# A graph network's fourth edge pass: one engine change per round, ten rounds per group, twelve buffers of gathered rows

## The reference, cut to what matters

```
proj_feat = (in_feat @ W_proj).reshape(n_nodes, n_head, d_out)
src_score = jnp.sum(proj_feat * a_src, axis=-1)
tgt_score = jnp.sum(proj_feat * a_tgt, axis=-1)
edge_score = leaky_relu(src_score[src_ind] + tgt_score[tgt_ind], negative_slope=0.2)
edge_score = jnp.exp(edge_score - jnp.max(edge_score))
neigh_sums = segment_sum(edge_score, tgt_ind)
att_per_edge = edge_score / (neigh_sums[tgt_ind] + 1e-16)
out_feat = segment_sum(proj_feat[src_ind] * att_per_edge[..., None], tgt_ind)
```

## Time and profile before

| what | value |
|---|---|
| median of 3 runs | 7075.83 us (7072.01 to 7086.69) |
| profiled execution | 7071.4 us, span 7069.7 us |
| busy in the span | TensorE 5276.6 us (75%), VectorE 4158.6 us (59%), GpSimd 4214.4 us (60%), ScalarE 2748.0 us (39%) |
| granted TensorE clock, mean | 0.883 |
| the pass `edges_3` | about 5848 to 6626 us of the span |

### The profile page before, as it was taken

The page is one execution under the profiler, slowest core; times in us unless marked ns, Lnnn a source line. Parts: engine busy times, 40 slices in busy tenths (PEclk is TensorE's granted clock), DMA queues, the critical chain, the costliest instruction groups (busy, mean ns, idle before and its releaser), DMA issues. The chain is left out here.

```text
span 7069.7 us, 108538 instructions
## 1 busy us (share of the span) xinstructions
PE 5276.6 (75%) x29030; PEld 3736.3 (53%) x29030; DVE 4158.6 (59%) x14866; ACT 2748.0 (39%) x6645; POOL 4214.4 (60%) x3907
## 2 busy tenths in 40 slices
PE   4776889788866665787699996766666675776788
PEld 3655677545455554333488874333333344555566
DVE  4454777523345555777488884544445454655698
ACT  0000555411111212666355554555555462222354
POOL 4664466666668886777644442455555445554598
PEclk9898999988888887999799998888888887888899
DMA  4554666444456666999545552333333332333466
GB/s 128 174 173 150 178 179 177 136 124 135 131 117 107 106 108 128 317 301 303 176 141 147 152 148 74 90 86 88 86 89 90 84 87 60 74 72 72 121 185 175
DMA packets 1163875, 966.37 MB, mean 137 GB/s; under 512 B 161046, under 2 KB 975586, under 8 KB 1163268
## 3 DMA queue, kind: packets, MB, share of 16 engines
q1 hardware_dynamic: 977956, 684.36, 32.2%
q0 software_dynamic: 163072, 210.16, 15.4%
q10 hardware_dynamic: 22240, 64.90, 2.5%
HBM read 485.30 MB, written 496.79 MB: 139 GB/s over the span
## 5 line engine op out<-in xcount | busy, mean ns | idle before, releaser
L2337 PE MATMUL l_nodes_f<-l_nodes_h_t_s,w_f 128*128 128x512 f32 x784 | 435.7, 684 | 433.4 <-ACT l_nodes_act_t L2289 422.9
L526 POOL DMA_INDIRECT tgt_tab<-l_nodes_ext,rank_at x392 | 389.9, 995 | 580.9 <-ACT l_nodes_ext L2312 474.0
L1556 POOL DMA_INDIRECT agg<-l_edges_b_rows,l_edges_b_at x392 | 608.5, 1552 | 133.9 <-issue 79.4
L1844 POOL DMA_INDIRECT l_edges_kv<-kv_tab,src_i x392 | 397.7, 1015 | 400.6 <-DVE l_edges_v_e L1865 291.2
L526 POOL DMA_INDIRECT to_col<-l_nodes_col_s,rank_row x392 | 415.4, 1060 | 326.6 <-ACT l_nodes_col_s L1250 232.3
L2510 POOL DMA_INDIRECT l_edges_proj<-proj_tab,src_i x392 | 382.3, 975 | 376.8 <-DVE l_edges_msg L2483 247.7
L435 POOL DMA_INDIRECT l_nodes_ag<-agg,sum_at x392 | 380.0, 969 | 241.4 <-issue 119.5
L961 POOL DMA_INDIRECT l_edges_fetched<-in_x,src_i x392 | 381.5, 973 | 218.8 <-DMA dst_i<-in_dst 111.0
L1314 POOL DMA_INDIRECT l_edges_a_at_row<-to_row,src_i x392 | 378.2, 965 | 219.0 <-issue 111.6
L526 POOL DMA_INDIRECT q_tab<-l_nodes_qkvs,rank_at x392 | 403.0, 1028 | 149.5 <-issue 105.9
L891 ACT COPY l_edges_rows<-l_edges_sums 128x264 f32<-128x264 f32 (+1 forms) x294 | 122.1, 450 | 947.9 <-DMA dst_i<-in_dst 463.7
(11 more groups left out here) (359 smaller groups left out, 14716.8 us busy)
## 6 DMA issues: line engine op xcount, KB each, us to landing
agg<-zeros ACTq DMA_DIRECT2D x98, 516.0 KB
l_nodes_xg<-x SPq DMA_DIRECT2D x196, 256.0 KB
kv_tab<-l_nodes_qkvs SPq DMA_DIRECT2D x98, 512.0 KB
agg<-l_edges_rows SPq DMA_DIRECT2D x98, 266.0 KB
l_nodes_ag<-agg SPq DMA_DIRECT2D x98, 266.0 KB
proj_tab<-l_nodes_ext SPq DMA_DIRECT2D x98, 264.0 KB
l_nodes_ag<-agg SPq DMA_DIRECT2D x98, 258.0 KB
l_nodes_ag_odd<-agg SPq DMA_DIRECT2D x98, 258.0 KB
```

What stands on the lines that cost most here:

```text
L526: pool.indirect_dma_start(table, bass.IndirectOffsetOnAxis(ranks[:, n * G + j:n * G + j + 1].bitcast(U32), 0), rows[:, j, :], None, bounds ...
L1556: pool.indirect_dma_start(agg1[j // 2], bass.IndirectOffsetOnAxis(at[k][:, j:j + 1].bitcast(U32), 0), rows[k][:, j, :], None, compute_op=A ...
L1844: pool.indirect_dma_start(kv[k][:, j, :], None, kv_tab, bass.IndirectOffsetOnAxis(src_i[:, n * G + j:n * G + j + 1].bitcast(U32), 0),).the ...
L2337: pe.matmul(f[m % 2][:], w_f1[:, m * P:(m + 1) * P], h_t_s[k][:], start=True, stop=True).then_inc(f_done, 1)
```

## The change

`edges_3` is rewritten with other lags and more buffers. No instruction that computes is added or removed; VectorE's, TensorE's, ScalarE's and GpSimd's counts for the pass stay the same.

- New lags: VectorE score 4, raise_top 5, lower 6, rest 1, one-hots 2, tail 2, marks, weigh and carry 7; TensorE total 8 (now first in its round), line 0, turn_top 4, spread_tgt 3, spread_top 5; ScalarE empty 9 (now first), line 1, middle 2, head 0, exponentials 6; SyncE's store 10.
- `proj` has twelve buffers (`DEEP`), and the gathers of group n wait for `weighed` of group n-12. `parts`, `lifted` and `msg` have four buffers, `both` one.
- VectorE's `weigh` loses its wait for `summed`; `spread_tgt` waits for `joined` of the group just before it rather than of the second before; the window's load waits for `rested` rather than `tgt_spread`.

```diff
-                proj = [sb(f"proj{k}", [P, G, D + H3]) for k in range(RING)]
-                parts = [sb(f"parts{k}", [P, G, 3, H3], BF16) for k in range(2)]
+                DEEP = 3 * RING
+                proj = [sb(f"proj{k}", [P, G, D + H3]) for k in range(DEEP)]
+                parts = [sb(f"parts{k}", [P, G, 3, H3], BF16) for k in range(RING)]
...
-                msg = [sb(f"msg{k}", [P, G, D + H3]) for k in range(2)]
+                msg = [sb(f"msg{k}", [P, G, D + H3]) for k in range(RING)]
...
                             dve.wait_ge(risen, n + 1)
-                            if follows(i, k, 2):
-                                dve.wait_ge(summed, n - 1)
-                            dve.tensor_tensor(msg[k % 2][:, :, 0:D].rearrange("p j (h c) -> p j h c", c=C3),
-                                              proj[k][:, :, 0:D].rearrange("p j (h c) -> p j h c", c=C3),
+                            dve.tensor_tensor(msg[k][:, :, 0:D].rearrange("p j (h c) -> p j h c", c=C3),
+                                              proj[n % DEEP][:, :, 0:D].rearrange("p j (h c) -> p j h c", c=C3),
...
-                        rotation(dve, groups, (1, take_rest), (2, score), (1, lambda i, k: mark_line(dve, i, k, tgt_spread)),
-                                 (1, take_tail), (2, raise_top),
-                                 (2, lambda i, k: mark(dve, i, k, (3, 2))), (2, lower), (2, lambda i, k: mark(dve, i, k, (1, 0))),
-                                 (2, weigh), (2, carry), loop=False)
+                        rotation(dve, groups, (4, score), (5, raise_top), (6, lower), (1, take_rest),
+                                 (2, lambda i, k: mark_line(dve, i, k, tgt_spread)), (2, take_tail), (7, lambda i, k: mark(dve, i, k)),
+                                 (7, weigh), (7, carry), loop=False)
...
-                            if reuses(i):
-
-                                pool.wait_ge(weighed, n - RING + 1)
+                            if n >= DEEP:
+
+                                pool.wait_ge(weighed, n - DEEP + 1)
                                 pool.sem_inc(pool_turn, 1)
...
-                            if follows(i, k, 2):
-
-                                pe.wait_ge(joined, n - 1)
+                            if follows(i, k, 1):
+
+                                pe.wait_ge(joined, n)
...
-                            if follows(i, k, 2):
-
-                                act.wait_ge(summed, n - 1)
+                            if n >= RING:
+
+                                act.wait_ge(summed, n - RING + 1)
...
-                        rotation(pe, groups, (2, turn_top), (0, lambda i, k: spread_line(pe, i, k)), (1, spread_tgt), (2, spread_top),
-                                 (3, total_messages), loop=False)
+                        rotation(pe, groups, (8, total_messages), (0, lambda i, k: spread_line(pe, i, k)), (4, turn_top),
+                                 (3, spread_tgt), (5, spread_top), loop=False)
...
-                        rotation(act, groups, (1, take_middle), (0, lambda i, k: copy_line(act, i, k)), (0, take_head), (2, rise), (2, ease_carry),
-                                 (3, lambda i, k: empty(act, i, k, low)), loop=False)
+                        rotation(act, groups, (9, lambda i, k: empty(act, i, k, low)), (1, lambda i, k: copy_line(act, i, k)), (2, take_middle),
+                                 (0, take_head), (6, rise), (6, ease_carry), loop=False)
...
-                        rotation(sp, groups, (0, lambda i, k: load_window(sp, i, k, tgt_spread)), (5, lambda i, k: store(sp, i, k)), loop=False)
+                        rotation(sp, groups, (0, lambda i, k: load_window(sp, i, k, rested)), (10, lambda i, k: store(sp, i, k)), loop=False)
```

More of the change, by code:

```diff
@@ L2413, in edges_3 @@
                 headed, rested, middled, tailed, joined = (sem(n) for n in ("headed", "rested", "middled", "tailed", "joined"))
-                proj_in = [[sem(f"proj_in{k}{j}") for j in range(G)] for k in range(RING)]
+                proj_in = [[sem(f"proj_in{k}{j}") for j in range(G)] for k in range(DEEP)]
                 with nc.Block() as block:
@@ L2448, in take_rest @@
                                 dve.wait_ge(tailed, n - 1)
-                            dve.tensor_tensor(rest[k % 2][:], tgt[k][:], parts[k % 2][:, :, 0, :], ALU.subtract).then_inc(rested, 1)
+                            dve.tensor_tensor(rest[k % 2][:], tgt[k][:], parts[k][:, :, 0, :], ALU.subtract).then_inc(rested, 1)
                         def take_tail(i, k):
@@ L2453, in take_tail @@
                             dve.wait_ge(middled, n + 1)
-                            dve.tensor_tensor(parts[k % 2][:, :, 2, :], rest[k % 2][:], parts[k % 2][:, :, 1, :],
+                            dve.tensor_tensor(parts[k][:, :, 2, :], rest[k % 2][:], parts[k][:, :, 1, :],
                                               ALU.subtract).then_inc(tailed, 1)
@@ L2521, in spread_tgt @@
                             pe.wait_ge(hot_made, n + 1)
-                            if follows(i, k, 2):
-                                pe.wait_ge(joined, n - 1)
+                            if follows(i, k, 1):
+                                pe.wait_ge(joined, n)
                             spread_rows(pe, lambda j: tgt_p[:, k % 2, j].rearrange("p s h -> p (s h)"), at_rank[k % 2],
-                                        parts[k % 2][:].rearrange("p t s h -> p t (s h)"), 3 * H3).then_inc(tgt_spread, 1)
+                                        parts[k][:].rearrange("p t s h -> p t (s h)"), 3 * H3).then_inc(tgt_spread, 1)
                         def turn_top(i, k):
@@ L2543, in total_messages @@
                             pe.wait_ge(weighed, place(i, k) + 1)
-                            total(pe, i, k, msg[k % 2])
-                        rotation(pe, groups, (2, turn_top), (0, lambda i, k: spread_line(pe, i, k)), (1, spread_tgt), (2, spread_top),
-                                 (3, total_messages), loop=False)
+                            total(pe, i, k, msg[k])
+                        rotation(pe, groups, (8, total_messages), (0, lambda i, k: spread_line(pe, i, k)), (4, turn_top),
+                                 (3, spread_tgt), (5, spread_top), loop=False)
                     @block.scalar
@@ L2553, in take_head @@
                             act.wait_ge(window_in[k], i * 16 + 16)
-                            if follows(i, k, 2):
-                                act.wait_ge(tgt_spread, n - 1)
-                            act.copy(parts[k % 2][:, :, 0, :], tgt[k][:]).then_inc(headed, 1)
+                            if n >= RING:
+                                act.wait_ge(tgt_spread, n - RING + 1)
+                            act.copy(parts[k][:, :, 0, :], tgt[k][:]).then_inc(headed, 1)
                         def take_middle(i, k):
@@ L2560, in take_middle @@
                             act.wait_ge(rested, n + 1)
-                            act.copy(parts[k % 2][:, :, 1, :], rest[k % 2][:]).then_inc(middled, 1)
+                            act.copy(parts[k][:, :, 1, :], rest[k % 2][:]).then_inc(middled, 1)
                         def rise(i, k):
@@ L2566, in rise @@
                             act.wait_ge(scored, n + 1)
-                            if follows(i, k, 2):
-                                act.wait_ge(summed, n - 1)
-                            act.activation(msg[k % 2][:, :, D:D + H3], lifted[k % 2][:], ACT.Exp, bias=low[k][:]).then_inc(risen, 1)
+                            if n >= RING:
+                                act.wait_ge(summed, n - RING + 1)
+                            act.activation(msg[k][:, :, D:D + H3], lifted[k][:], ACT.Exp, bias=low[k][:]).then_inc(risen, 1)
                         def ease_carry(i, k):
```

21 lines of the change are left out of this document (11 added, 10 removed).

## The result

The changed kernel takes 7126.22 us (median of 4 runs, 7119.97 to 7131.42) against 7073.92 us: 1.0072 of the kernel before, 95% interval 1.006 to 1.0085. It is slower, by 52 us; the forecast was 7034 us with a range from 6880 to 7125. Two later sets of runs gave 1.0084 (1.0058 to 1.0111) and 1.0079 (1.0055 to 1.0103).

A forecast was written before the change was run, and what follows sets the result against it. Late TensorE results during outstanding gathers, not an engine, bound edges_3. A 50 us later start, 85 groups at 6.95 us and 64 us at the end gave -42 us: 7029 profiled, 7034 us median with 4.4 us added; range 6880 to 7125.

The forecast's parts named there:

- What bounds the pass: edges_3: no engine; some 2.5 of each 7.7 us waiting, TensorE's results reaching readers late until outstanding gathers land.
- that pause: Second layer's edge pass: after a string of twelve gathers the next starts 3.99 us later, released by a matmul.
- The rule of the Trainium skill: Cited against the reading: TensorE's ports are shared with no one, DMA has its own, so gathers cannot obstruct matmuls.
- The start: Start of edges_3: 48 gathers at once put the first weigh near 5920, 50 us later, after one long wait.
- The end: Last 12 groups of edges_3, with no gathers to trigger: 12 x 5.35 = 64 us.
- The pace: The 85 groups between start and end: R taken as 6.95 us each, from three or four groups per release.
- the sum of the prediction: Change in edges_3's time: 85 R - 633 us, break-even at R = 7.45, -42 us at R = 6.95.
- the slow round: VectorE's round after a release, at TensorE's low clock: 7.3 us against 5.35; deeper buffers were to make it rarer.
- Rival D: Slower: two groups per release in edges_3, R = 8.0, +47 us, 7123 us; chance 0.26.
- The strings are as dense as before: GpSimd's fetch credit: a weigh still buys exactly four gathers, so data is early but strings are not shorter.
- What follows the pass: After edges_3's last weigh: total, stores and next pass were taken to stay as before.
- Rival B: Engines bind edges_3, results on time or lateness covered: R = 5.35, -178 us, 6898 us; chance 0.20.

The follow-up runs named there:

- pool_direct: The changed kernel with indirect gathers replaced by direct loads of consecutive (wrong) rows that GpSimd still issues: 6756.0 us, 0.9550 of the kernel before.
- sync_plain: The changed kernel with gathers replaced by plain loads of consecutive (wrong) rows from SyncE's queue, twelve buffers: 6791.3 us, 0.9600 of the kernel before.
- before_pad: The kernel before with eight unused tensors allocated in the edge pass: 6057.0 us, 0.9998 of the kernel before, in the set without late results.
- before_depth12: The kernel before with twelve buffers of gathered rows and their credit, nothing else changed: 7101.5 us, 1.0021 of the kernel before.
- before_head_credit: The kernel before, old lags, with twelve buffers and gathers also waiting for group n-2's score sum: 0.9986 without late results, 0.9973 (6963.4 us) with them.
- head_credit: The changed kernel, gathers also waiting for group n-4's score sum (first six groups: a tail): 6038.4 us, 0.9969 without late results; 6837.0 us, 0.9809 with them.

## Why the prediction was wrong, step by step

**What bounds the pass: right in the main.** That TensorE's results arrive late while gathers are outstanding was a reading of a few rows; plain loads took the lateness away and gave the forecast times within 7 us. Two parts of the reading did not hold. The second layer's gathers of the earlier trace rows can wait for their own string through a matmul that needs its data, so that pause proves nothing by itself. And that results are let go when the string has landed fits most releases but not all: at 6217.50, above, one came 1.0 us after the last issue, before any landing on record (2.6 us at least), and at 5897.15, below, one came while the string of 48 ran on. The rule of the Trainium skill, "SBUF — State Buffer", section "Who interferes with whom", speaks of ports, and no row here shows a port. With gathers outstanding L870's 20 records took 2.52 us, as in the earlier trace rows. But TensorE was held up beside them in another way, which I overlooked. In the changed kernel it sits idle between the matmuls and weight loads of L876, which behind the first wait for nothing of another engine; in 33 of 84 groups their 8 records, 1.06 us long elsewhere, take over 2.2. From the waits shown above:

```profile
PEld l_edges_sums L876 <- issue: 90.9, 124, 1.4
PE l_edges_sums L876 <- issue: 64.7, 96, 1.2
```

In the kernel before the first of these is 3.0 us in 13 waits, and in pool_direct, sync_plain and before_pad neither stands there. So what comes late is not only the news of TensorE's ends, and whoever takes the section to say that gathers cannot hold TensorE up is corrected by these rows.

**The start: right in size.** Forecast 50 us, measured 51.2. The depth is what costs it, for before_depth12 in the old lags loses 44 us by its fourth weigh. In the new lags, with seven rounds ahead of the first weigh, it shows as two long waits of VectorE, not the one I described, and the second ends 6.4 us after the last issue, not 2.2 to 2.4. The changed kernel's timeline at the start:

```profile
5897.15 0.21 DVE L2423 TENSOR_REDUCE l_edges_whole<-l_edges_tgt_p 128x16 f32<-128x48 f32 x1 [24.61 <-DMA l_nodes_ag<-agg,sum_at]
...
5919.61 0.95 POOL L2509 DMA_INDIRECT l_edges_proj<-proj_tab,src_i  x1 [0.30 <-issue]
5925.97 0.21 DVE L2423 TENSOR_REDUCE l_edges_whole<-l_edges_tgt_p 128x16 f32<-128x48 f32 x1 [26.05 <-DMA l_nodes_ag<-agg,sum_at]
```

**The end: better than forecast.** Forecast 64 us for the last twelve groups, measured 54.3, since the new order runs at 4.7 to 6.7 us in the first seven of them and at 2.9 to 4.4 in the last five, as its lists empty.

**The pace: the step that failed.** "With m groups per release ... I take 6.95, between the second and the fourth" rested on the count of groups per release staying at three or four. It is two, with 8.35 us. With that pace in the sum of the prediction, 85 x 8.35 - 633 = +77 us; the shorter end (10 us) and node pass (20 us) and the later first gather (12 us) bring it to the +60 of the table. I argued that the total at the head of TensorE's round makes the slow round rarer. What it does is to put the three small results that VectorE's next round begins with behind 3.6 to 6.3 us of total, late in a string of eight, where they are held to its end. Rival D had the two groups per release and the chance 0.26. Its cycle of 4.4 + 5.35 + 6.2 = 16 us took 17.1 in the one that starts at 6217.50: 4.8, 4.8 and 7.5, the last because the string of eight (6223.09 to 6231.96) and 2.64 us behind it set the release. That its time, 7123 us, is 3 us from the median is luck: a pace 0.35 us too low is 30 us, and the last twelve groups and the node pass made up for just that.

**"The strings are as dense as before": wrong, but not by depth.** A weigh still buys four gathers, yet with two weighs 4.8 us apart their gathers always join: 38 strings of eight where there were 25. Twelve buffers alone do not do it, as before_depth12 has 17 of eight, 45 of four and a pace of 7.78 us.

**What follows the pass: missed.** The node pass, untouched by the change, takes 414 to 418 in place of 435 us in every kernel with eight or twelve buffers but before_head_credit, which takes 429 and 430. Tensors' places are not the reason (before_pad, 435.2). In it GpSimd is busy 392 of 415 us; why it falls into this rhythm stays open.

**Rival B** failed under the hold. Without it only relatives ran: sync_plain with 4.98 us per group, head_credit with 5.25 against 5.36; the changed kernel itself, with its gathers, was never run without the hold.

## What to carry to other kernels

When a consumer starts long after its producer's record ends, look for what ends at that moment on the other engines, then replace that one thing by a plain form: here that gave the cost (240 us of this pass) at once. Where a late signal waits for a string of transfers, more buffers make the first string longer (44 us here) and gain no pace; give the credit at the head of the consumer's round, so that each string of transfers is short and ends before the next result is needed. Read the intervals one by one before you trust a mean, for one long interval at the start of a pass looks like a slower pace. And put the results that another engine waits for ahead of the long work in a round, after seeing what that order makes wait in its turn.

## What the runs showed of the hardware

With GpSimd's indirect gathers outstanding, TensorE's ends reached VectorE and ScalarE late, and VectorE sat up to 33 us for one (before_depth12); with as many direct loads from GpSimd or SyncE, none did. In the changed kernel TensorE itself stood between the weight loads of L876, 90.9 us in 124 waits. The hold is not always there: in one set of six, the only one on its chip, the same kernel had no late end and took 6057 us in place of 6968 to 7082. What differs there was not found, and the pages of the profile name no cause. Such waits appear as waits for a DMA of another pass, which is the sign to look for.
